# A decoder layer pair: loading and converting the shared expert's weights two turns later beside the second attention core

## What is computed

```
x = _layernorm(x + _L1_attn_ref(x, L1_attn_Wq, ...))          # called core D here
x = _layernorm(x + _L1_xattn_ref(x, ctx_2048, ctx_2048))      # core E: q = x, k = v = ctx, no projections
# _L1_ffn_ref:
shared = (silu(x @ Sg) * (x @ Su)) @ Sd                       # FS = 704 hidden columns
shared = sigmoid(x @ Wsg) * shared
out = moe_out + shared
```

## Time and profile before

| | |
|---|---|
| median of 3 runs | 784.97 us (783.76 to 786.84) |
| the profiled execution | 786.64 us, of which 784.9 from its first to its last instruction (the span) |
| busy: PE, DVE, ACT, POOL | 684.0 (87%), 561.3 (72%), 489.8 (62%), 251.3 (32%) |
| mean granted TensorE clock | 0.922 of 2.4 GHz |
| transfers | 95.61 MB, 122 GB/s over the span |

### The profile page before, as it was taken

One profiled execution on the slowest core, in us unless ns is written; L12 is line 12 of the kernel. 1 busy time (PEld: TensorE's weight loads), 2 busy tenths in 40 slices (PEclk: granted clock), 3 DMA queues, 4 the chain that ended last, 5 costly groups with the idle time before them and its releaser, 6 DMA issues.

```text
span 784.9 us, 18601 instructions
## 1 busy us (share of the span) xinstructions
PE 684.0 (87%) x4914; PEld 612.1 (78%) x4915; DVE 561.3 (72%) x2515; ACT 489.8 (62%) x1354; POOL 251.3 (32%) x422
## 2 busy tenths in 40 slices
PE   5889799678864988999997999998799989999982
PEld 5888577544434988999997999997689978888882
DVE  4788588767887547888885997997666665555486
ACT  4546576467771329899996997995345545555443
POOL 3443200323335400122221221223055415555554
PEclk9999899957685999999998998999799999999996
DMA  9940000000003686677775675651034523333162
GB/s 292 359 136 1 0 1 1 1 0 2 0 1 108 195 296 186 197 200 208 206 215 146 194 195 140 166 152 38 2 105 142 164 67 107 95 99 100 43 236 80
DMA packets 66489, 95.61 MB, mean 122 GB/s; under 512 B 11390, under 2 KB 52992, under 8 KB 66304
## 3 DMA queue, kind: packets, MB, share of 16 engines
q1 hardware_dynamic: 63024, 86.51, 37.2%
q0 software_dynamic: 3408, 8.43, 3.0%
HBM read 62.45 MB, written 33.36 MB: 122 GB/s over the span
## 4 chain that ended last, share of the span: by engine, by line
PE 44%; issue 17%; DVE 16%; SPq 9%; ACT 6%; DMA 4%; POOL 2%; DVEq 0%; ACTq 0%; POOLq 0%
PE bank L1905 8%; PE bank L2047 5%; SPq L494 5%; PE bank L1981 5%; PE bank L1891 5%; PE bank L1637 4%; PE bank L2071 3%; PE bank L1998 3%; SPq L490 3%; PE bank L1880 2%; PE bank L2035 2%; PE bank L1921 2%; PE bank L1802 1%; PE bank L1831 1%; DVE bank L1373 1%
## 5 line engine op out<-in xcount | busy, mean ns | idle before, releaser
L937 ACT ACTIVATE late_mem<-bank,smax 128x128 f32<-128x128 f32 x512 | 149.7, 401 | 15.3 <-DVE smax L1373 13.4
L1373 DVE CUSTOM_DVE_ANT_0 bank<-bank,causal 128x128 f32<-128x128 f32 x512 | 132.8, 323 | 21.2 <-issue 19.8
L1905 PE MATMUL bank<-f_mem,late_mem 128*128 128x68 f32 (+3 forms) x1024 | 130.7, 272 | 0.2
L1905 PEld LDWEIGHTS bank<-f_mem,late_mem 128*128 128x128 f32 x1024 | 127.7, 196 | 0.8 <-POOL f_mem L675 0.6
L613 POOL TENSOR_TENSOR rstd<-var,power 128x2 f32<-128x2 f32 (+1 forms) x64 | 40.3, 630 | 194.2 <-DVE var L1112 179.2
L1891 PE MATMUL bank<-ident,late_mem 128*128 128x128 f32 x512 | 80.6, 281 | 7.8 <-ACT late_mem L937 7.3
L947 ACT ACTIVATE late_mem<-bank 128x512 f32<-128x512 f32 x128 | 81.3, 635 | 7.8 <-PE bank L1891 6.9
L1373 DVE DVE_READ_ACCUMULATOR2_ANT smax<- 128x1 f32 x512 | 72.4, 141 | 0.0
L1891 PEld LDWEIGHTS bank<-ident,late_mem 128*128 128x128 f32 x512 | 60.4, 144 | 10.8 <-ACT late_mem L937 10.7
L1880 PE MATMUL bank<-kz,qs 128*128 128x256 f32 x256 | 64.9, 337 | 2.2 <-DMA kz<-k_E 1.3
L1981 PE MATMUL bank<-x_hi,w_hi 128*128 128x256 f32 x176 | 51.6, 293 | 1.0 <-DVE x_lo L1431 1.0
(11 more groups left out here) (283 smaller groups left out, 2013.1 us busy)
## 6 DMA issues: line engine op xcount, KB each, us to landing
qs<-q_D SPq DMA_DIRECT2D x64, 128.0 KB, 2.7
kz<-k_D SPq DMA_DIRECT2D x128, 64.0 KB, 2.5
qs<-q_E SPq DMA_DIRECT2D x64, 128.0 KB, 2.7
kz<-k_E SPq DMA_DIRECT2D x128, 64.0 KB, 2.4
xg<-f_mem SPq DMA_DIRECT2D x1, 5031.0 KB, 22.6
late_mem<-xg SPq DMA_DIRECT2D x39, 129.0 KB, 2.0
q_D<-stage_d SPq DMA_DIRECT2D x8, 512.0 KB, 2.9
k_D<-stage_d SPq DMA_DIRECT2D x8, 512.0 KB, 4.0
```

The costliest lines, as they stand in the source:

```text
L937: ins = sc.activation(sp[:, g, i, :], bank[g][:, i * P:(i + 1) * P], ACT.Exp, bias=smax[:, g, i:i + 1], scale=-1.0)
L1373: ins = ve.tensor_tensor_reduce(v[:, i, :], v[:, i, :], causal[:, :], -1.0, 3e38, ALU.add, ALU.min, smax[:, g, i:i + 1])
L1905: ins = mm(bank[6][:, h * (DH + 1):to * (DH + 1)], spt[:, g, i, :], vf[:, slot, h:to, :].rearrange("p h d -> p (h d)"), start=True, stop=True)
```

## The change

The two conversion steps get a lag of 2 turns, and SP's step gives the slice of two turns earlier: slice t is loaded in SP's step 16 + t (before: 14 + t) and converted in turn 18 + t (before: 16 + t). In the 18th and later steps all orders within a turn stay. TensorE's and POOL's instructions and all waits' conditions are the same.

```diff
@@ SP, the loop over steps s
-                t = s - B + 2
+                t = s - B
                 if 0 <= t < B:
                     load_w(t)
@@ ACT, stages of the cores
                 if g == 0:
-                    stages += [(LAG_XP, e_high, None), (0, None, w_high)]
+                    stages += [(LAG_XP, e_high, None), (2, None, w_high)]
@@ DVE, stages of the cores
                                     (4, d_apply, e_apply), both(3, 0, softmax), (1, heads_out("D"), heads_out("E")),
-                                    (0, None, w_low)])
+                                    (2, None, w_low)])
```

## The result

The changed kernel took 775.46 us (median of 4 runs, 774.44 to 777.27) beside 784.4 for the kernel before (4 runs): a ratio of 0.9898, 95% interval 0.9861 to 0.9936. By the ratio that is 8.0 us faster, between 5.0 and 10.9 (by the two medians 8.9). Forecast were 778.9, a gain of 6.1, in a range of 775.5 to 783.2; the measured time lies on the lower edge of that range. A second measurement (experiment 5), with 11 runs, gave a ratio of 0.9958 (0.9935 to 0.9982), a gain of 3.3 us, between 1.4 and 5.1. Both belong to the result: the two intervals only touch, at about 5 us, and why the measurements differ is looked at in the experiments and stays open in part.

The account below looks back on a forecast made before the run. TensorE held 44% of the chain; ACT's wait stalled it in turn 16, and SP paced the next turns. Gain 6.45 less 0.36 at the second core's end, 6.1 us from 784.97, gave 778.9, range 775.5 to 783.2.

Parts of the forecast that it names:

- The wait of ACT: Turn 16: w_high(0) waits for the last keys store; moved to turn 18, TensorE alone would be 7.45 us earlier.
- SP's queue: SP's stack of row 3 starts 6.45 us earlier and paces the turns to 24; 1.0 of 7.45 becomes SP's wait.
- The end of core E: End of the second core: w_low(14) now stands before the score copy and delays the chain; loss 0.36 us.
- The clock: TensorE's 4 us gap goes, but late stacks in turns 17 and 18 could halve the clock; a fall costs 2.8 us.
- The fall of turn 24 goes away: Rival: turn 24's halved clock does not recur; gain 6.1 + 2.8 = 8.9, so 776.1 us; chance 0.2.
- A new wait takes part of it: Rival: a late row 1 or 2 stack pauses TensorE in turns 17 or 18, clock falls; 781.7 to 783.2; chance 0.19.
- Slower: Rival: SP, without its rest, delivers turns 17 to 24's stacks late, the clock falling each time; 790.1 us; chance 0.03.

Follow-up runs that it names:

- experiment 5: The changed kernel measured again, on one chip with two kernels that store the keys early, with a new trace; 778.25 us, ratio 0.9958.
- Experiment 1: The changed kernel with ACT again waiting in turn 16 for the last keys store, converting nothing there; 782.34 us, ratio 1.0006.
- experiment 3: The kernel before, with keys stored early (two rows in each of SP's steps 0 to 3, one in steps 4 to 11); 775.12 us, ratio 0.9896.
- experiment 6: The kernel before with the keys stored early, measured again on one chip with a new trace; 774.91 us, ratio 0.9914.
- experiment 4: The changed kernel with the keys stored early as well; 777.28 us, ratio 0.9933.
- experiment 8: The kernel before, unchanged, traced again; one run, 780.15 us.
- experiment 7: The changed kernel with the keys stored early as well, measured again on one chip with a new trace; 776.98 us, ratio 0.9939.
- experiment 2: Loads and conversions one turn later than in the kernel before, instead of two; 777.24 us, ratio 0.9925.
- experiment 9: The changed kernel with two small extra transfers issued by SP in each of steps 16 to 22; 786.24 us, ratio 1.0046.
- keys early alone: The kernel before with keys stored in SP's steps 0 to 11, loads and conversions unmoved; measured twice, 775.12 and 774.91 us.

## Why the prediction was right, point by point

**The wait of ACT: right.** The forecast said that `w_high` at turn 16 waits for the last `keys` store and for nothing else that matters. Experiment 1 brings the whole time back with the wait alone, experiments 3 and 6 remove it at its source. The size: 7.45 us forecast for turns 16 and 17 together. The kernels with the stall and without differ by 117.37 - 110.10 = 7.27 (experiment 1 against experiment 4, which have the same order of conversions; the second also has the keys early).

**SP's queue: the mechanism was right, the term mis-sized.** The step "SP is then the later of the two: 424.85 in place of 431.30, 6.45 us earlier", of which 1.0 of 7.45 was SP's to keep. By traces with no fall of the clock after turn 17, "turns 17 to 31" take 117.4 and 117.9 us with the stall (experiments 1 and 8) and 112.1 in the changed kernel: 5.2 to 5.7. SP kept 1.8 to 2.0, as experiments 3 to 7 show with the keys early. SP's start of row 3's stack was as forecast (6.78 us behind the stack before it, for 6.48). Two things were missing. Row 2's stack, whose arrival the forecast took as in time, came late: it starts 6.47 us behind turn 16's pair (416.39 - 409.92) where it was 5.92 (418.37 - 412.45), turn 18's first scores wait 0.46 for it, and turn 17 takes 8.20 us in place of 7.49. And a slow issue: one `kz` of eight took about 1.3 us more in the very step that had no slack left (5.04 us for the group in one trace, 5.10 in the other), and turn 19's first scores waited 1.40 and 0.98 for it. So the pair of turn 18 stood 15.69 us behind that of turn 16, not 15.0, and turn 18 took 7.98 where the kernel of experiment 3 takes 6.78. It was no accident, and the old trace had it: the `qs` group of that same stack takes 2.69 us there where others take 1.71, and the `kz` group of row 5's stack 4.74. It belonged into the term and not only into the range.

**The end of core E: as forecast in its place, smaller in its sum.** The score copy came 0.35 later, forecast 0.36. From the second pair of turn 31 to the shared expert's first product took 20.39 us before and 20.46 now. Over all traces it is 20.14 to 20.51 (mean 20.36) in the four with the conversions in their old place, 20.46 to 20.75 (mean 20.66) in the six with them two turns later, and 20.50 in experiment 2: 0.3 on the mean, with a scatter as large. The clock goes to 0.50 there in every trace, 10 to 13 us behind turn 31's pair, which may be the source of the scatter; that isn't shown. The router loads were issued at 533.94; no wait for them was seen.

**The clock: right that it could go either way, too small a price.** A fall was priced at 2.8 us from one turn. Counted with the wait ahead of it, it cost more: the pairs of turns 23, 24 and 25 of the first old trace stand at 472.09, 481.49 and 490.02, so 9.40 and 8.53 us where experiment 1's took 7.31 and 7.17, 3.45 more, and turns 20 and 21 of the changed kernel took 3.65 more than in its other trace (3.4 over the whole core). Two rivals rested on it, and something like each was seen once. "The fall of turn 24 goes away" is the first pair of traces: 5.6 + 4.0 = 9.6 (with 0.5 of it in turn 22). But the change did not remove that fall: experiments 1 and 8 have the stall and no such fall, so it belonged to one execution. "A new wait takes part of it" is the second trace of the change, a wait of 1.29 us and a fall behind it, though in turn 21 and not in 17 or 18 as the rival had it. So the two measured gains of 8.0 and 3.3 us lie on the two sides of the forecast, and the turns without falls say 5.2 to 5.7 less 0.3 at the end, about 5. That the first time came out inside the range, on its edge, and that the second gain is the second rival's 3.3, is in part luck. That the falls cause the whole difference between the two measurements is argued from two traces of each kernel, not shown: a time without a trace doesn't tell where its clock fell.

**Slower** did not come about for the change, and experiment 9 shows its mechanism: with two issues more a step the waits and two falls (one of them behind a wait for ACT) ate the gain and more, 1.0046.

The best of these kernels is keys early alone (0.9896 and 0.9914; the changed kernel's first 0.9898 is as low, its second, measured beside it on the same chip, is not): the source of the wait is removed, SP no longer waits for stores between stacks, and nothing is put into the chain at the end of core E.

## What to carry to other kernels

When a step waits for something that another engine does late, read which engine's queue paces the work behind the stall before pricing its removal: the gain is the smaller of what the stall costs and what that queue can follow. Moving the waiting step hides the wait; moving the work that it waits for to where its queue has room removes it, here also for the queue itself. And take two traces of a kernel before a single slow turn is priced or promised: it may be an accident of one execution, as the fall of turn 24 was, or come back every time, as the slow issue did.

## What the runs showed of the hardware

The granted clock fell to 0.50 (1.2 GHz) behind each of the three stalls of TensorE in turn 16 (4.13, 3.78 and 3.97 us). Behind shorter waits it fell in some executions and not in others: it fell behind 0.73 (the first trace of the kernel before), 1.29 (experiment 5) and 2.29 and 1.29 us (experiment 9), and stayed at 1.00 behind 0.74 (experiment 8), 1.03 and 1.51 (experiment 2), 1.36 (experiment 9) and 1.40 (turn 19 of the changed kernel). With waits of at most 0.60 in core E, four traces of two kernels have no fall. The length of the last wait alone doesn't decide it; what else it depends on is open.

One `kz` issue in a group of eight took 1.0 to 1.7 us more of SP than the usual 0.42, and it comes back in the same stacks: in all eleven traces the `kz` group of core E's row 5 takes 4.63 to 5.18 us and that of row 4 3.66 to 3.69. In row 3's stack it is there in all seven traces without the stall that have no added transfers (4.68 to 5.32). Its cause wasn't looked for.
